# Layer 2's normalisations and weight split run in pieces inside layer 1's combining loop; the last stage's beginning is reordered

## The reference, cut to what matters

```python
# layer 1, second half: a routed mixture of 64 experts, 8 per token
h = _layernorm(x, axis=-1) * (1 + cb) + sb
x = x + gb * _L1_ffn_ref(h, ...)        # ends in out.at[tok].add(y * w[:, None])
# layer 2, first half
h = _layernorm(x, axis=-1) * (1 + ca) + sa
x = x + ga * _L2_attn_ref(h, ...)       # begins with h = _layernorm(x, ln1w, ln1b), then h @ Wq, h @ Wk, h @ Wv,
                                        # a causal convolution with 4 taps, silu, and three more products
# layer 3, second half, the last part
logits = clip(xt @ gate_w.T, -50, 50); top_w, top_idx = top_k(logits, 2); rw = softmax(top_w)
deltas = softmax(expert_atom_weights) @ atoms; weighted = deltas * sigmoid(importance)
vals = einsum('tk,tks->ts', rw, weighted[top_idx])
out = xt @ W.T + segment_sum((xt[:, cols] * vals).T, rows).T
```

## Time and profile before

| | us |
|---|---|
| median of 3 runs (lowest, highest) | 1727.04 (1724.38, 1731.39) |
| the profiled execution's own time | 1726.34 |
| its span in the trace | 1724.5 |
| PE busy | 1566.7 |
| DVE busy | 989.1 |
| ACT busy | 813.0 |
| POOL busy | 369.0 |

### The profile page before, as it was taken

One profiled execution on the slowest core, in us unless ns is written; L12 is line 12 of the kernel. 1 busy time (PEld: TensorE's weight loads), 2 busy tenths in 40 slices (PEclk: granted clock), 3 DMA queues, 4 the chain that ended last, 5 costly groups with the idle time before them and its releaser, 6 DMA issues. The chain is left out here.

```text
span 1724.5 us, 26924 instructions
## 1 busy us (share of the span) xinstructions
PE 1566.7 (91%) x8967; PEld 1261.3 (73%) x8968; DVE 989.1 (57%) x2339; ACT 813.0 (47%) x1779; POOL 369.0 (21%) x402
## 2 busy tenths in 40 slices
PE   8999999996729999887969988989999999999997
PEld 7687576864628989675726876867888898888665
DVE  4477262344555654224385354567777777777476
ACT  4677232332324555104675353346655566555443
POOL 3300001211066666573001221230000000000000
PEclk8999978998759999658989998999999999999899
DMA  3000030151615666332001015320000000000100
GB/s 135 13 13 1 25 132 10 46 137 37 270 52 170 187 187 185 112 106 87 1 0 28 27 47 147 93 82 19 20 18 1 18 18 18 16 2 0 48 0 25
DMA packets 56170, 109.32 MB, mean 63 GB/s; under 512 B 9937, under 2 KB 37457, under 8 KB 54458
## 3 DMA queue, kind: packets, MB, share of 16 engines
q1 hardware_dynamic: 45874, 82.10, 14.9%
q0 software_dynamic: 9168, 25.05, 5.2%
q10 hardware_dynamic: 1040, 1.05, 0.2%
HBM read 89.39 MB, written 18.78 MB: 63 GB/s over the span
## 5 line engine op out<-in xcount | busy, mean ns | idle before, releaser
L1731 POOL DMA_INDIRECT h_modulated<-l1f_rows,ln_rstd x127 | 119.8, 943 | 61.9 <-PE bank L1798 55.6
L2890 ACT ACTIVATE l_mem<-bank 128x129 f32<-128x129 f32 x240 | 66.4, 278 | 114.9 <-PE bank L2716 114.8
L1818 PE MATMUL bank<-l1f_up,l1f_wt 128*128 128x192 f32 x508 | 105.3, 331 | 0.0
L2606 POOL COPY l_sg<-l_keys 128x512 f32<-128x512 f32 x32 | 24.7, 772 | 375.8 <-DVE l_keys L3003 375.8
L2716 PE MATMUL bank<-l_dr,l_nkt 128*128 128x129 f32 x480 | 99.9, 293 | 1.3 <-DVE l_dr L3048 0.7
L2728 PE MATMUL bank<-l_mem,l_sg 128*128 128x129 f32 x480 | 95.4, 290 | 1.9 <-ACT l_mem L2890 0.5
L2629 PE MATMUL bank<-h_modulated,l_wo 128*128 128x128 f32 x512 | 92.2, 283 | 0.6 <-DVE h_modulated L2987 0.6
L3048 DVE SCALAR_TENSOR_TENSOR l_dr<-bank,l_inv,l_v 128x128 f32<-128x128 f32 x240 | 84.3, 351 | 8.5
L1861 PE MATMUL bank<-l1f_wt,ln_square 128*128 128x128 f32 x256 | 72.7, 444 | 13.6 <-DMA ln_square<-l1f_y_rows,l1f_back_at 11.7
L329 ACT ACT_TABLE_LOAD x10 | 12.8, 1283 | 150.0 <-PEq L88 150.0
L1818 PEld LDWEIGHTS bank<-l1f_up,l1f_wt 128*128 128x128 f32 x508 | 81.0, 193 | 0.1
(11 more groups left out here) (617 smaller groups left out, 4376.7 us busy)
## 6 DMA issues: line engine op xcount, KB each, us to landing
l1f_y_rows<-h_modulated SPq DMA_DIRECT2D x127, 128.0 KB, 1.9
l1f_up<-in_l1f_up SPq DMA_DIRECT2D x8, 1536.0 KB
l_w<-in_l_w SPq DMA_DIRECT2D x9, 768.0 KB, 4.3
l1f_down<-in_l1f_down SPq DMA_DIRECT2D x4, 1536.0 KB, 21.6
wmod<-in_wmod SPq DMA_DIRECT2D x3, 1536.0 KB, 11.5
l2e_w<-in_l2f_win SPq DMA_DIRECT2D x14, 256.0 KB, 2.8
l_w<-in_l_wqk SPq DMA_DIRECT2D x8, 256.0 KB, 2.8
l0m_w<-in_l0f_win SPq DMA_DIRECT2D x8, 256.0 KB, 2.7
```

The costliest lines, as they stand in the source:

```text
L1731: pool.indirect_dma_start(xg[:, i % GETS], None, table, bass.IndirectOffsetOnAxis(ap=listing[:, ORDER[i]:ORDER[i] + 1], axis=0)).then_inc( ...
L1818: last = pe.matmul(k.bank[:, UP + i % 2, 0:2 * F], xt[:, i % 2, b], of_owner(up, i)[:, :, b, :], start=(b == 0), stop=(b == DB - 1))
L2890: act.activation(mem[:, a, (n + 1) % 2, 0:W1], k.bank[:, MEM + a, 0:W1], ACT.Identity).then_inc(s["mem_copied"], 1)
```

## The change

It has two parts that do not touch each other.

1. A class `PieceNorm` does what `LayerNorm` does, one piece at a time and each engine's share in a function of its own. The combining loop of `l1_experts` now runs over 82 steps instead of 64. In the steps `16 + 16q` and on, piece q of both normalisations is worked through (`place_of`): as soon as the tiles 2q and 2q + 1 of `k.x` are complete, the mean, the variance and so on of that piece are put between the combining products, each at a fixed step r behind 16 + 16q. The last piece runs in the steps 64 to 81, in which there is nothing left to combine, with idle products between. PSUM is shared out anew: combining uses 4 banks in place of 8. SP loads `cols`, `w` and `wo` after the last row of `y_rows` is stored, ACT rounds the weights in 2 parts, and DVE forms `w_lo` in 6 parts in the steps 12 to 17 (before: POOL, in one). Their buffers (`Front`) lie where the experts' `down` weights lay. `l2_attention` starts with the projections at once; its first two blocks are gone.
2. In `l3_ffn` the transfers are issued in another order, the softmax of the atoms runs inside the normalisation, the logits wait for half of the tokens at a time, PE does two dense products, two deltas and a third dense product before the transposes, ACT takes the softmaxes before `h_hi`, DVE does `colf`, `h_lo` and `rowf` later, and three of the four parts of the low values (`low_values`) move into the first pair of the loop.

```diff
+class PieceNorm:
+    def mean(self, pe, p):
+        if p >= 2:
+            pe.wait_ge(self.s["root_ready"], p - 1)
+        self.sums(pe, p, 0, self.src, self.s["mean_ready"])
+    def var(self, pe, p):
+        pe.wait_ge(self.s["squared"], p + 1)
+        self.sums(pe, p, 1, self.sq, self.s["var_ready"])
+    def center(self, dve, p):
+        dve.wait_ge(self.s["mean_ready"], p + 1)
+        dve.tensor_tensor(... ALU.subtract).then_inc(self.s["centered"], 1)
+    def square(self, act, p): ...
+    def root(self, act, p): ...
+    def scaled(self, dve, p):
+        dve.wait_ge(self.s["root_ready"], p + 1)
+        for b in (1, 0):
+            dve.scalar_tensor_tensor(...).then_inc(self.s[f"scaled_b{b}"], 1)
+        dve.wait_ge(self.s["scaled_b0"], p + 1)
+        dve.tensor_scalar(... ALU.add).then_inc(self.s["out_b0"], 1)
+    def shifted(self, act, p): ...
...
 def l1_experts(k, norm, experts, front):
+        LN_FROM, LN_EACH, LAST_STEP = 2 * TOP, 2 * TOP, 2 * TOP * 5 + 2
+        def place_of(step):
+            return [(q, step - LN_FROM - q * LN_EACH) for q in range(PieceNorm.PIECES)]
...
             def _(sp):
+                sp.dma_start(front.cols, d["l2_cols"]).then_inc(s["front_cols_in"], 16)
+                sp.dma_start(front.w, ...).then_inc(s["front_w_in"], 16)
+                sp.dma_start(front.wo, ...).then_inc(s["front_wo_in"], 16)
...
             def _(pe):
-                    if j == 0 and t >= 4:
-                        pe.wait_ge(s["x_added"], t - 3)
+                    if j == 0 and t >= 2:
+                        pe.wait_ge(s["x_added"], t - 1)
-                pe.wait_ge(s["x_added"], TT - 3)
-                k.idle_products(pe, 1, 0)
+                for step in range(LAST_STEP):
+                    if step < TT * TOP:
+                        combine(step)
+                    for q, r in place_of(step):
+                        if r == 2:
+                            pe.wait_ge(s["x_added"], 2 * q + 2)
+                            adaln2.mean(pe, q)
+                        elif r == 5:
+                            adaln2.var(pe, q)
+                        elif r == 9:
+                            adaln2.wait(pe, q)
+                            norm1.mean(pe, q)
+                        elif r == 12:
+                            norm1.var(pe, q)
+                        if step >= TT * TOP and r in (2, 5, 9, 12):
+                            k.idle_products(pe, 1, 0)
...
             def _(act):
+                # after the last expert tile: w_hi in two parts, then for each step:
+                # r == 5 square, 6 root, 8 shifted (adaln2); 11 square, 12 root, 14 shifted (norm1); 15 h_hi
...
             def _(dve):
+                for step in range(LAST_STEP):
+                    if TOP + 4 <= step < TOP + 4 + W_LO:
+                        split_w(step - TOP - 4)
+                    for q, r in place_of(step):
+                        if r == 1 + LN_EACH:
+                            split_h(q)
+                        elif r == 5:
+                            adaln2.center(dve, q)
+                        elif r == 8:
+                            adaln2.scaled(dve, q)
+                        elif r == 11:
+                            norm1.center(dve, q)
+                        elif r == 14:
+                            norm1.scaled(dve, q)
+                    if step < TT * TOP:
+                        weigh_for(step)
+                    if step % TOP == TOP // 2 and TOP < step <= TT * TOP + TOP // 2:
+                        add_tile(step // TOP - 1)
...
 def l3_ffn(k, norm):
@@ PE
-                norm.wait(pe)
                 for t in range(TT):
+                    if t % (TT // NCH) == 0:
+                        norm.wait(pe, t // (TT // NCH))
-                dense(0)
                 pe.wait_ge(s["ea_ready"], 1)
                 pe.transpose(k.bank[0:A, 1, 0:E], ea[:], k.ident[0:E, 0:E]).then_inc(s["eat_ready"], 1)
+                dense(0)
                 dense(1)
+                pe.wait_ge(s["eat_copied"], 1)
+                deltas(0)
+                deltas(1)
+                dense(2)
                 pe.wait_ge(s["weights_ready"], 1)
                 # eight transposes of m3
-                pe.wait_ge(s["eat_copied"], 1)
-                deltas(0)
-                deltas(1)
-                dense(2)
                 deltas(2)
                 deltas(3)
                 dense(3)
@@ DVE
+                norm.on_vector(dve, softmax_of_atoms)
...
-                for n in range(N // CH):
-                    dve.wait_ge(s["val_hi_ready"], n + 1)
-                    dve.tensor_tensor(val_all[LOW_VAL, chunk(n)], ...).then_inc(s["val_split"], 1)
-                dve.wait_ge(s["val_split"], N // CH)
+                low_values(0)
...
                             if not (final and unit):
                                 make_pick(i, unit + 1)
+                        if first and n:
+                            low_values(n)
```

More of the change, by code:

```diff
@@ L1603, in l1_experts @@
+def l1_experts(k, norm, experts, front):
     nc, d = k.nc, k.dram
@@ L1853, in _, with combine @@
                 down_products(TILES - 1)
-                for g in range(TT * TOP):
+                def combine(g):
                     t, j = divmod(g, TOP)
@@ L3451, in build @@
             if n == 2:
+                with ExitStack() as front_ctx:
+                    front = Front(k, front_ctx)
                 experts = Experts(k, experts_ctx)
+            if n == 4:
+                with k.stage():
+                    part(k, front)
+                experts_ctx.close()
+                continue
             with k.stage(), ExitStack() as norm_ctx:
```

260 lines of the change are left out of this document (162 added, 98 removed).

## The result

| | us | against before |
|---|---|---|
| before, in the same session | 1727.03 median (1724.38 to 1731.39, 4 runs) | |
| after | 1707.69 median (1701.90 to 1710.75, 4 runs) | 0.9897, 95% interval 0.9864 to 0.9929 |
| after, timed again later | 1706.03 median (1699.63 to 1714.2, 6 runs) | 0.9887, 95% interval 0.9855 to 0.9919 |
| after's profiled execution | 1701.9, span 1700.2 | 24.4 under that of before |

By these ratios the changed kernel is 17.8 us (12 to 23) faster, 19.5 us when timed again. The forecast was 14.7 us (1712), with 1705 to 1721 as its range.

A forecast was written before the change was run, and what follows sets the result against it. PE was taken to set the pace, busy 91% of the span, except where it waits or is slow. Gains of 12.2 (layer 2) and 2.5 us (last stage) made 14.7, from 1726.34 to 1711.6, so 1712; range 1705 to 1721.

The forecast's parts named there:

- the forecast's own band: Whole kernel: the time lies between 1708.5 and 1717 us; chance 0.54.
- the first rival: Combining loop: PE's clock stays up through the pieces, PE is 1.3 us late, time 1706.5 to 1708.5; chance 0.14.
- PE's lateness: End of the combining loop, step 63: PE lags POOL's pace by 4 us over three pieces; ends 1.3 and 9.
- The last piece's way: Last addition to first projection: 0.75 hand-over, 13.0 for two normalisations, 2.7 for the halves and the stage's end.
- a piece costs PE 19.1 us at 2.4 GHz: Combining loop: 16 steps of 0.71, four sums of 0.92 and 4.1 us of waits, against POOL's 20.0.
- the mean of 21.3: Combining loop: PE's cost per piece between 19.1 at 2.4 GHz and 25.1 at 1.2 GHz, 1.3 us over POOL's pace.
- The holes in it: Combining loop: PE waits for DVE's weight matrix 1.4 us at r = 8, 0.6 at r = 11, 2.1 at r = 14.
- the price at the low level: Combining loop at 1.2 GHz: steps of 1.01 us, sums of 1.7, so 25.1 us of PE per piece.
- the third rival: Combining loop: DVE's scalings collide with POOL's gathers, 12 scalings cost 27 us, time 1739; chance 0.06.
- PE stays at 1.2 GHz: Combining loop: PE ends 15.3 us late, nothing is gained at layer 2, time 1725; chance 0.11.
- Part 2: Last stage's beginning: the reordering gains 2.5 us, ends 0.5 and 4.5.
- The first `up`: Last stage: it starts 3.0 us earlier, from logits ending 0.9 earlier and a hole 1.7 us shorter.

The follow-up runs named there:

- e5: The changed kernel without the four idle products between the last piece's sums; 1710.05 us, ratio 0.9918.
- e10: The changed kernel with PE running each sum of the first three pieces twice; 1711.58 us, ratio 0.9898.
- after_again: The changed kernel itself, unchanged, timed and traced again; 1706.03 us, ratio 0.9887.
- e1: The changed kernel with the last stage's beginning as before, so layer 2's part alone; 1714.08 us, ratio 0.9924.
- e6: The changed kernel with all four subtractions of low values ahead of the last stage's pairs again; 1709.42 us, ratio 0.9913.

## Why the prediction was right, and where its terms were off

The result of 1707.69 lies below the forecast's own band (1708.5 to 1717) and in that of the first rival (1706.5 to 1708.5); it is inside the range because that rival was in it. The term that put it there is PE's lateness.

**The last piece's way** was 16.45 by the sum and 16.42 by the trace, as 0.66, 6.97, 6.00 and 2.79 for 0.75, 13.0 and 2.7. One sum of four was cold (2.08 us). This rests on the idle products: without them it is 19.3 (e5).

**PE's lateness** is the term that failed: 4 us were charged, and there is practically none. From the last gather's start to the last addition it is 786.73 - 782.48 = 4.25 us, and it was 788.14 - 784.02 = 4.12 before. The step that failed is "a piece costs PE 19.1 us at 2.4 GHz" and the mean of 21.3 drawn between it and 25.1. The holes in it were right (1.59, 0.62, 2.16 for 1.4, 0.6, 2.1). But 0.71 us for a step is the price of four records that wait for their gather; in a run they take less: 12 records 1.76 us and 20 records 2.52, so 0.50 to 0.59 a step. With 0.5, a piece costs 8 + 3.7 + 4.4 = 16.1 us at 2.4 GHz (an estimate from these rows), against 20.0 of POOL.

In the changed kernel the matrix behind r = 14 ends a hole at 744.76, 765.18 and 785.56; of each 20.4 us between them PE waits 0.9 and 0.8 for gathers, so a piece with its low stretch costs PE 19.5 us where the sum had 21.3. e10 tests it: with four more sums (3.7) a piece should take 19.8, and its two warm pieces are 20.1 and 19.8 us apart, where the prediction's price would give 22.8.

And the price at the low level mattered less than the mean had it: behind each of the first two pieces the clock was low (0.50 and 0.65 from 746 to 754, 0.56 and 0.59 from 766 to 774), beginning in steps in which PE waited for gathers, and it was 1.00 where the holes are. So it caught up in each piece. The lateness is that of the first rival, "PE stays fast", but not for its reason: the clock did fall back once a piece, as the forecast had it, and over 725 to 792 us it was 0.82, between the 0.6 to 0.8 of the forecast and the 0.9 of that rival.

**The gathers** cost 1.6 us that the sum did not have (80.5 for 78.9). That is a small case of the third rival the other way round: DVE's operations hold the gathers, the scalings among them (1.03 us for 0.95 at 776.09), and are not held themselves. The scalings stand at 482 ns in the loop too:

```profile
L1679 DVE SCALAR_TENSOR_TENSOR h_modulated<-h_modulated,modulation,l1f_up x8: 476/482/485, 734.9 to 793.4; 128x256 f32<-128x256 f32 x8
```

The Trainium skill (SBUF — State Buffer, Who interferes with whom) has a DMA issued from GpSimd starve of descriptor generation under DVE operations that take the shared port pair, and says that a probe did not see a `tensor_tensor` stall one. The traces agree that gathers are held, but differ on the kind: 0.95 us became up to 1.40 (e5) beside a `tensor_tensor` with two SBUF inputs.

Together: to the first projection 12.2 us were forecast and 14.5 came (115.6 to 101.2): 3.9 more from PE's lateness, less 1.6 for the gathers. In after_again and e1 it was 13.2 and 13.3, as one more sum of the tail ran cold. A further 1.0 us came behind the first projection in the changed kernel's first trace (275.0 - 101.2 = 173.8 for 174.9) and not in e1 (174.8) or after_again (174.9). That too is the clock: over the two first stretches of 4 us of the projections it is 0.61 and 0.96 in the changed kernel, 0.50 and 0.76 to 0.78 in e1 and after_again. So some 2 of the 15.5 us come and go from one execution to the next, and the changed kernel's first trace was lucky in both places.

**PE stays at 1.2 GHz**, the second rival, is refuted by the stretches: from 734 to 746 the clock is 1.00 over holes of 1.59, 0.62 and 2.16 us. The Trainium skill (TensorE: Matmul & The Clock Gate, HAM oscillation) describes a loop in which each wait for a transfer is long enough to throttle the array again, so that the next burst starts cold. No hole of the loop here did that within a piece, and where the clock was at 0.50, from 746 to 750, PE's longest hole was 0.37 us. The prediction had named that page for its second rival; what it describes is another case.

**Part 2** was forecast at 2.5 us and is 5.2 in the two profiled executions, with the right mechanism throughout. The first `up` was to start 3.0 earlier and starts 4.0 earlier. The hole gives 1.7, as worked out (3.37 to 1.66). The logits start 1.05 us sooner after the stage's start (9.60 for 10.65), for 0.9. The rest, 1.3, lies in PE's own run from there to the last dense product, which takes 17.55 us for 18.82, where the forecast had 0.5. The first pair was to take 0.5 of this back (1.0 for the low values, less 0.5 for the clock), and gave 1.2 more instead (74.2 us from first `up` to final additions for 75.3): a warm first pair is worth 75.3 - 73.5 = 1.8 (before against e1), not 0.5, and the low values in it cost 74.16 - 73.52 = 0.6, not 1.0. The term that was mis-sized most is the clock's.

**In sum**, against the 14.7 forecast the two traces' changed stretches show 15.5 + 5.2 = 20.7, and the times 17.8 and 19.5. The errors were of one sign except the gathers'.

## What to carry to other kernels

A loop that a slow transfer engine paces is a place to put another stage's work, and the test of how much it takes is the engine's price in an unbroken run, not in a run of waits; the mean of a group in which the engine waits overstates it. In this loop PE was slow in stretches in which it had slack, and at full clock in the pieces that made it late, so the lateness did not add up over the pieces; but the first piece after a slack stretch was paid partly at the low clock (5.3 us late in e10, and hardly made up later). Before two traces are compared, measure the change inside its own stage, since here unchanged stages differ by as much as the gain.

## What the runs showed of the hardware

- TensorE's clock stayed at 2.4 GHz over a hole of 3.37 us in one execution (e1) and fell in a hole of the same length in another (before: 0.77 and 0.63 us for the records behind it, 0.47 and 0.40 in e1). With the new order and a hole of 1.66 it was up in the changed kernel; behind 3.81 (e6) it fell.
- In all ten traces with the new order of the last stage and the low values in the first pair, the stage takes 102.9 to 103.0 us. With the old order it takes 108.2 to 109.3, by where its clock falls (three traces). So part of a gain can be that a chance is removed.
- The length of PE's holes does not tell the clock's level. In the loop of before no hole was longer than 1.2 us and the clock was 0.54 on the mean; from 734 to 746 us of the changed kernel it was 1.00 over holes of up to 2.16.
- Indirect gathers of 128 rows took 0.95 us. All 87 of the 896 in these traces that took over 0.955 (up to 1.40) began while a DVE operation without a PSUM input was running, and ended 0.81 to 0.82 us after its end. Why the `tensor_scalar` ones held only some of the gathers beside them is open.
